# The up projection's fourth chunk by rounded parts, and GpSimd's tile instructions joined

## The reference

```python
# per sample: adapter of its language, with residual and layer norm
h = relu(x @ W1[lang] + b1[lang])                 # 512x512 by 512x128: "up"
y = x + h @ W2[lang] + b2[lang]                   # 512x128 by 128x512: "down"
norm = (y - mean(y)) * rsqrt(var(y) + 1e-5)
x1 = x + norm * gamma[lang] + beta[lang]
# linear layer of its category, with residual
out = x1 + x1 @ W[cat] + b[cat]                   # 512x512 by 512x512: "linear"
```

## Time and profile before

| | |
|---|---|
| Median of 3 runs | 619.06 us (618.46 to 619.56) |
| Profiled execution: its time | 617.23 us |
| Profiled execution: span from first to last instruction | 615.4 us |
| TensorE matmuls busy | 607.9 us (99% of the span) |
| TensorE weight loads busy | 491.7 us (80%) |
| VectorE busy | 523.1 us (85%) |
| ScalarE busy | 510.9 us (83%) |
| GpSimd busy | 548.1 us (89%) |
| Granted TensorE clock, mean | 1.000 |
| DMA | 166.25 MB, 270 GB/s |

### The profile page before, as it was taken

One profiled execution on the slowest core, in us unless ns is written; L12 is line 12 of the kernel. 1 busy time (PEld: TensorE's weight loads), 2 busy tenths in 40 slices (PEclk: granted clock), 3 DMA queues, 4 the chain that ended last, 5 costly groups with the idle time before them and its releaser, 6 DMA issues.

```text
span 615.4 us, 10928 instructions
## 1 busy us (share of the span) xinstructions
PE 607.9 (99%) x2888; PEld 491.7 (80%) x2888; DVE 523.1 (85%) x1154; ACT 510.9 (83%) x769; POOL 548.1 (89%) x442
## 2 busy tenths in 40 slices
PE   9999999999999999999999999999999999999998
PEld 7767888788887878888888888887888888888887
DVE  1799798889898888998888898889898889898673
ACT  4768888988888888888888888888888888889770
POOL 3789999999999999999999999999999999999930
PEclk9999999999999999999999999999999999999999
DMA  8968898898998888988888998888998898897422
GB/s 304 261 199 270 306 305 274 262 292 271 307 304 257 275 279 281 317 272 290 274 281 275 314 286 271 284 275 275 315 292 273 281 297 259 305 306 272 157 85 103
DMA packets 125761, 166.25 MB, mean 270 GB/s; under 512 B 10883, under 2 KB 72589, under 8 KB 121633
## 3 DMA queue, kind: packets, MB, share of 16 engines
q1 hardware_dynamic: 94756, 150.12, 74.6%
q10 hardware_dynamic: 30972, 15.78, 9.1%
HBM read 132.17 MB, written 33.55 MB: 269 GB/s over the span
## 4 chain that ended last, share of the span: by engine, by line
PE 66%; POOL 13%; ACT 9%; issue 5%; DVE 4%; DMA 2%; ACTq 0%; POOLq 0%; DVEq 0%
PE o_bank L822 13%; PE o_bank L820 13%; PE o_bank L821 13%; PE n_bank L838 6%; ACT norm L483 5%; POOL xs_lo L385 5%; PE d_bank L851 4%; PE d_bank L820 4%; PE d_bank L822 4%; PE d_bank L821 4%; DMA x_quad<-in_x 2%; POOL w_raw L396 2%; POOL w_lo L372 2%; POOL w_lo L412 2%; PE y_bank L820 2%
## 5 line engine op out<-in xcount | busy, mean ns | idle before, releaser
L820 PE MATMUL o_bank<-w_hi,x1T_hi 128*128 128x512 f32 x512 | 205.1, 401 | 0.7 <-DVE x1T_lo L716 0.7
L822 PE MATMUL o_bank<-w_hi,x1T_lo 128*128 128x512 f32 x512 | 200.0, 391 | 0.0
L821 PE MATMUL o_bank<-w_lo,x1T_hi 128*128 128x512 f32 x512 | 199.1, 389 | 0.0
L406 POOL TENSOR_TENSOR x_tok<-x_tok,b_bc 128x512 f32<-128x512 f32 x128 | 164.4, 1312 | 11.5 <-DMA b_bc<-in_L_cond_b 6.8
L412 POOL TENSOR_TENSOR w_lo<-w_raw,w_hi 128x512 fp32r<-128x512 f32 x128 | 163.6, 1306 | 9.9 <-ACT w_hi L493 9.9
L483 ACT ACTIVATE norm<-y,neg_mean_rstd,rstd 128x512 f32<-128x512 f32 x127 | 151.4, 1270 | 1.1 <-DVE neg_mean_rstd L701 1.1
L651 DVE STREAM_TRANSPOSE xT<-x_quad 128x512 f32<-128x512 f32 x120 | 126.7, 1103 | 29.9 <-DMA x_quad<-in_x 29.9
L822 PEld LDWEIGHTS o_bank<-w_hi,x1T_lo 128*128 128x128 f32 x512 | 96.1, 188 | 20.9
L820 PEld LDWEIGHTS o_bank<-w_hi,x1T_hi 128*128 128x128 f32 x512 | 96.3, 188 | 19.2 <-issue 1.3
L821 PEld LDWEIGHTS o_bank<-w_lo,x1T_hi 128*128 128x128 f32 x512 | 96.4, 188 | 18.0
L385 POOL TENSOR_TENSOR xs_lo<-xT,xs_hi 128x512 fp32r<-128x512 f32 x87 | 110.5, 1302 | 0.0
(11 more groups left out here) (85 smaller groups left out, 804.6 us busy)
## 6 DMA issues: line engine op xcount, KB each, us to landing
w_raw<-in_L_cond_W SPq DMA_DIRECT2D x32, 1024.0 KB, 6.5
out<-out_half SPq DMA_DIRECT2D x63, 512.0 KB, 3.8
x_tok<-in_x SPq DMA_DIRECT2D x31, 1024.0 KB, 11.2
w_raw<-in_L_cond_W SPq DMA_DIRECT2D x64, 256.0 KB, 4.2
b_bc<-in_L_cond_b SPq DMA_DIRECT2D x64, 256.0 KB, 8.6
x_quad<-in_x SPq DMA_DIRECT2D x62, 256.0 KB, 3.7
x_quad<-in_x ACTq DMA_DIRECT2D x58, 256.0 KB, 10.5
x_tok<-in_x ACTq DMA_DIRECT2D x2, 256.0 KB, 3.3
```

The source lines that it names most:

```text
L406: pool.tensor_tensor(x_tok[p][:, t, :], x_tok[p][:, t, :], b2_bc[p][:, :], ALU.add).then_inc(x_b2_done, 1)
L820: pe.matmul(acc, lhs_hi, rhs_hi, start=first, stop=False)
L821: pe.matmul(acc, lhs_hi, rhs_lo, start=False, stop=False)
L822: return pe.matmul(acc, lhs_lo, rhs_hi, start=False, stop=last)
```

## The change

- NS becomes 4. The fourth chunk of the up projection is split like the others: TensorE's plain matmul gives way to three split ones; ScalarE's roundings of W1 and x transposed, and GpSimd's subtractions for them, take in four chunks and no longer three. `up` waits once for all of `xs_lo`.
- GpSimd's `low_xs` is one instruction over 128x2048 in place of three over 128x512. From step 2 on, `plus_b2` and `low_w` are done in pairs of tiles: one instruction over 128x1024 in place of two over 128x512.
- One b2 tile is left (and at the start `b_bc[1]` holds sample 1's b2). So its load has to wait until the sums of the step have read it: it moves behind the load of b and the first store in SyncE's order, with a wait for `x_b2_done`.
- The zeros for `keep_clock` lie in an output tile.

```diff
-    NS = 3
+    NS = 4
@@ tiles
-        b2_bc = [sb(f"b2_bc{i}", [P, H]) for i in range(2)]
+        b2_bc = sb("b2_bc", [P, H])
-        zeros = sb("zeros", [P, P])
+        zeros = out_half[1][:, 1, 0:P]
+        def b2_of(k):
+            return b_bc[1] if k.since(1) and not k.since(2) else b2_bc
@@ SyncE, step
                 if loads:
-                    load_b2(lang, q)
                     load_x(k.sample(-1), q)
...
                 if linear:
                     store(k, 2, 0)
                 if loads:
+                    sp.wait_ge(x_b2_done, k.count(NT, 0, NT))
+                    load_b2(lang, q)
                     sp.wait_ge(x1_lo_done, k.count(NC, 0, 0))
                     load_params(lang, q)
@@ GpSimd
                 pool.wait_ge(xs_hi_done, k.count(1, 1, 0))
-                for c in range(NS):
-                    pool.tensor_tensor(xs_lo[:, c, :], xT[(k.x + 1) % 3][:, c, :], xs_hi[:, c, :].bitcast(F32),
-                                       ALU.subtract).then_inc(xs_lo_done, 1)
+                pool.tensor_tensor(xs_lo[:, :, :], xT[(k.x + 1) % 3][:, 0:NS, :], xs_hi[:, :, :].bitcast(F32),
+                                   ALU.subtract).then_inc(xs_lo_done, 1)
...
+                def plus_b2_pair(t):
+                    if t == 0:
+                        pool.wait_ge(x_in[p], 16 * k.pairs(0) + 16)
+                        pool.wait_ge(b2_in[p], 16 * k.pairs(0) + 16)
+                    pair = x_tok[p][:, t:t + 2, :]
+                    pool.tensor_tensor(pair, pair, b2_of(k)[:, :].rearrange("p (o h) -> p o h", o=1
+                                       ).to_broadcast([P, 2, H]), ALU.add).then_inc(x_b2_done, 2)
+
+                def low_w_pair(c):
+                    pool.wait_ge(w_hi_done, k.count(2, 1, c // 2 + 1))
+                    pool.tensor_tensor(w_lo[q][:, c:c + 2, :], w_raw[q][:, c:c + 2, :],
+                                       w_hi[q][:, c:c + 2, :].bitcast(F32), ALU.subtract).then_inc(w_lo_done, 2)
@@ GpSimd, step (from step 2 on)
                     if adapter:
-                        plus_b2(0)
-                        plus_b2(1)
+                        plus_b2_pair(0)
                     if turn:
-                        low_w(0)
-                        low_w(1)
+                        low_w_pair(0)
                     if adapter:
-                        plus_b2(2)
-                        plus_b2(3)
+                        plus_b2_pair(2)
                     if turn:
-                        low_w(2)
-                        low_w(3)
+                        low_w_pair(2)
@@ TensorE, up
                 if parts:
                     pe.wait_ge(w1_lo_done, k.count(1, 2, 0))
+                    pe.wait_ge(xs_lo_done, k.count(1, 3, 1))
                 for c in range(parts):
-                    pe.wait_ge(xs_lo_done, k.count(NS, 3, c + 1))
                     ins = split_product(acc, w1_hi[:, c, :], w1_lo[:, c, :], xs_hi[:, c, :], xs_lo[:, c, :],
-                                        False, c == parts - 1)
+                                        c == 0 and parts == NC, c == parts - 1)
```

More of the change, by code:

```diff
@@ L252, in load_w2, with load_b2 @@
                              ).then_inc(w2_in[p], 16)
-            def load_b2(lang, p):
-                sp.dma_start(b2_bc[p][:, :], b2[bass.ds(lang, 1)].to_broadcast([P, H])
+            def load_b2(lang, p, dst=b2_bc):
+                sp.dma_start(dst[:, :], b2[bass.ds(lang, 1)].to_broadcast([P, H])
                              ).then_inc(b2_in[p], 16)
@@ L326, in _ @@
             lang1 = sample_id(0, 1, L)
-            load_b2(lang1, 1)
+            load_b2(lang1, 1, b_bc[1])
             load_w1(lang1, 1)
@@ L405, in plus_b2 @@
                             pool.wait_ge(first_xT_turned, k.count(NC, 0, NC))
-                    pool.tensor_tensor(x_tok[p][:, t, :], x_tok[p][:, t, :], b2_bc[p][:, :],
+                    pool.tensor_tensor(x_tok[p][:, t, :], x_tok[p][:, t, :], b2_of(k)[:, :],
                                        ALU.add).then_inc(x_b2_done, 1)
+                def plus_b2_pair(t):
[9 more added lines that the diff above has]
+                                       w_hi[q][:, c:c + 2, :].bitcast(F32), ALU.subtract).then_inc(w_lo_done, 2)
                 def low_w(c):
@@ L634, in _ @@
             STATS = 5
-            dve.memset(zeros[:, :], 0.0).then_inc(zeros_done, 1)
+            dve.memset(zeros, 0.0).then_inc(zeros_done, 1)
             dve.memset(spare[:, 0:1], 0.0).then_inc(out_done, OUT_CREDIT)
@@ L827, in keep_clock @@
                 for _ in range(count):
-                    pe.matmul(idle_bank[:, 0:P], zeros[:, :], zeros[:, :], start=True, stop=True)
+                    pe.matmul(idle_bank[:, 0:P], zeros, zeros, start=True, stop=True)
             def turn_norm(k, c):
```

## The result

The changed kernel takes 647.62 us (median of 5 runs, 646.65 to 647.99) against 619.4 us for the kernel before (median of 5, 618.46 to 619.64): a ratio of 1.0456, 95% interval 1.0439 to 1.0473. It is slower by 28 us. The forecast was 653.0 us, the range 642 to 661. (The forecast was worked from a median of 619.06 us for the kernel before.) The profiled execution took 647.99 us, its span is 646.2.

The account below looks back on a forecast made before the run. A closed GpSimd-ScalarE ring of waits, tied with TensorE, was taken as the bound. It grows 0.29 + 0.92 = 1.21 us in 29 steps: 619.06 + 35.1, less 1.2 given back, gives 653.0 us, range 642 to 661.

Parts of the forecast that it names:

- What bounds the kernel: Whole kernel: two paths, GpSimd with ScalarE and TensorE's own step, tie within 0.1 us; both must shorten to gain.
- The ring: Closed path of waits, GpSimd from `low_w2` to `plus_identity`, ScalarE from `high_w` to `high_w2`: 18.45 us a step, growing to 19.66.
- TensorE's 0.17 us: Up projection: one plain matmul of 0.86 us out, three split of 0.23 in; 0.17 us less per step, 4.9 us in all.
- `low_w1`, +0.29 us: GpSimd, on the ring: 384 to 512 columns, costing like `low_w2`, 1.27 us for 0.97; +0.29 us a step.
- `low_xs` in one, +0.92 us: GpSimd, on the ring: one 2048-column instruction holds it 4.67 us, three of 512 held it 3.75; bounds +0.59 and +1.25.
- The ring's other parts: Steps that wait for TensorE now: the ring may run at 18.41 us instead of 18.45, giving 1.2 us back.
- Ends: Starting parts in the first 35 us, once each: costed at nothing, with up to 1 us either way.
- The b2 row at nothing: b2 load on SyncE, now behind the sums and the store: landing taken as 12.2 us, cost taken as nothing.
- the b2 ring: Sums, load, sums on one b2 tile: 19.6 us, as long as the ring; rival that it is longer, chance 0.08.
- The pairs at nothing: GpSimd's joined `plus_b2` and `low_w`: save 0.4 us a step where it waits for ScalarE anyway, so no gain.
- What would show it: Signs in the profile after: `low_xs` 4.7 us, step about 19.6, idle GpSimd 1.3, ScalarE 2, TensorE 1.4 us.
- TensorE's 614 us: Rival: TensorE sets the pace or the ring doesn't grow, so 4.9 us come out, 614.2 us; chance 0.06.

Follow-up runs that it names:

- the ring broken: Identity's sum moved straight behind the low part of W2: in the kernel before 616.43 us, ratio 0.9958; in the changed kernel 611.58 us, ratio 0.9882.
- the second experiment: Changed kernel with the b2 sums and the low parts of the linear weights made one tile at a time again: 647.66 us, ratio 1.0474.

## Why the prediction was right, point by point

- **What bounds the kernel.** Right. The ring and TensorE tie: the runs with TensorE's part alone (ratio 0.9992) and with the ring broken (0.9958) each gained little in the kernel before, both together (in the changed kernel, with its joins) 1.2%.
- **TensorE's 0.17 us.** Right in size (4.7 us between two runs, 4.9 worked out) and in that it can't be had behind the ring.
- **`low_w1`, +0.29 us.** It took 1.27 us for 0.97: +0.30.
- **`low_xs` in one, +0.92 us.** It was +0.85: 4.60 us where 4.67 had been worked out by the two widths of rows 7. The middle was the right choice between the bounds of 4.34 and 5.00, and a little too dear: 29 x 0.07 = 2.0 us of the error. The Trainium skill, "GPSIMD Engine Reference", section 3.1, has 4497 ns for such an instruction; the record here is 4641 ns on average. The page's figure was 3% short, the row's (4.73 us as a record) 2% long. The 647 us that the prediction worked out from the page is nearer to the result than its own 653.0, but by luck: 4.45 us for an instruction that took 4.60 is 4.4 us too little in 29 steps, and that made up for what the forecast had too high elsewhere (the next two points).
- **The ring's other parts.** I took 0.04 us a step back, for waits on TensorE that would vanish. It was more. From the identity's sum to the next `low_w2` the changed kernel takes 341.22 - 328.87 = 12.35 us; before, it was on average 18.45 less the 5.99 of rows 5 (312.52 - 306.53), 12.46. That is 0.11 us, so 0.07 more than I took, or some 2 us over the steps. Irregular steps such as that of 18.61 us in rows 5 didn't occur any more.
- **Ends.** The first full step began 1.1 us later (49.22 against 48.09), just outside the 1 us that I gave the start. Span against span the change cost 30.8 us where 33.9 was forecast. The mean step grew by 1.02 us and not by 1.17, which takes 4.2 off in 28 steps; the start adds 1.1; and what follows the last `low_w2` grew by 1.1 (50.8 to 51.9 us), about what I had put on a 29th step. The medians are 28.2 apart: the profiled execution of before was 2.2 us under its own median, that of the changed kernel 0.4 over.
- **The b2 row at nothing.** Right in the result for the changed kernel, but not in its working. I had let the landing be 12.2 us, the store's, so that the b2 ring tied with the other; and my lower bound of 9.2 us, said to be that of the b rows, is the mean of one b2 load and one b load (7.3 and 11.1 us), which the view puts in one line. Asked by line, the times from issue to landing of the b2 load before (L255), of the b load before (L267) and of the b2 load after (L259) are:

```profile
DMA to landing us min/median/max: 4.1/7.7/9.0
DMA to landing us min/median/max: 3.3/11.4/12.5
DMA to landing us min/median/max: 3.6/10.6/11.7
```

With 10.6 us the b2 ring of the changed kernel is about 18 us, well under 19.47, and had nothing to do with the result. Taken alone in the kernel before, the row cost 2 us. The load that is queued last didn't take longest. Why it took less than the store is not shown: size can't be all of it, as the b load, no larger than the b2 load, took 11.4 us before.

- **The pairs at nothing.** Right, to 0.04 us in the second experiment; GpSimd's idle time was their cover (1.32 us, forecast 1.3).
- **What would show it.** ScalarE's idle time before `high_w` is 1.97 us (2 forecast). TensorE's matmuls wait 30.7 us over 30 steps, 1.0 each, and its weight loads 1.4; forecast was 1.4.
- **The rivals.** TensorE's 614 us fell with the first trace. Its price of 4.9 us was about right (4.7 between two runs), but it could be had only once one instruction had been moved, in another kernel than this one.

## What to carry to other kernels

An engine's idle time hides only work that doesn't stand between two waits of the same closed path. Follow the path round once, engine by engine, add up its parts, and compare it with the busiest engine's own sum; if they tie, shorten the ring first, and do it by moving what nobody on the ring needs (here the subtractions) behind what somebody waits for (the identity's sum), before anything is added. Then the saving on the busiest engine is worth what its rows say, and the joined instructions are too, as far as their engine's own sum of work is what sets the step.

## What the runs showed that I had not expected

- With the ring broken in the changed kernel, GpSimd's records became longer, not its pace: `low_w2` 1358 ns on average for 1301, `low_xs` 4698 for 4641, while from the start of `low_w2` to the next instruction it was 1.26 us as before. A record's length is no measure of what it holds the engine; start to start is.
- Three 512-column instructions into one of 1536 save 0.27 us (3.75 to 3.48), and four into one of 2048 save 0.43 (5.03 to 4.60): 0.13 to 0.14 us for each instruction less, where two widths had given 0.11.
